# Reciprocals of an attention softmax spread over partitions by two transfers, their product moved to GpSimd, and keys spread by 8 transfers

## Chip, cores and metric

One core of one Trainium2 chip. The metric is the device time of one execution in microseconds (us), as the median of several runs.

## What is computed

Cross-attention with 16 heads of width 8 over sequences of 64 tokens (128 of them, 8192 tokens of width 128, all f32), added to its input, and then a feed-forward layer in which each token goes to the one expert of eight (each 128 to 512 to 128) that its logits choose.

```
x = x + _L0_xattn_ref(_layernorm(x), ctx, ctx, Wq, bq, Wk, bk, Wv, bv, Wo, bo)
x = x + _L0_ffn_ref(_layernorm(x), Wr, br, W1, b1, W2, b2)

q, k, v = heads(Q @ Wq.T + bq), heads(K @ Wk.T + bk), heads(V @ Wv.T + bv)
probs = softmax(einsum('bhqd,bhkd->bhqk', q, k) / sqrt(8))
out = einsum('bhqk,bhkd->bhqd', probs, v) @ Wo.T + bo

expert_idx = argmax(xf @ Wr.T + br)
h = relu(einsum('td,efd->etf', xf, W1) + b1)
y = einsum('etf,edf->etd', h, W2) + b2      # of the expert chosen
```

## The kernel before

Every engine has its own program, written out by hand; they meet at semaphores, and nothing reorders them. There are three stages.

**Stage 1** (0 to about 69 us) goes over 16 groups of 512 tokens (4 tiles of 128) and makes QT and KT (width on the partitions) and V.

**Stage 2** goes over 64 tiles in steps n, skewed by hand: in step n the scores of tile n are made, and older tiles are carried on. On TensorE a step is `scores(n)` (L877), the first four transposes of the exponentials of tile n-2 (L918) into bank 4, then small products, then the last four transposes into the same bank 4, which must wait until ScalarE has copied the first four out (L529), then the products with V (L994) and the sums of the exponentials (L1003) of tile n-3. VectorE takes the maximum (L698) and subtracts it (L706), ScalarE exponentiates (L546). GpSimd writes V out block by block (`VP`, L451) and sends routed rows to memory (L466, one indirect DMA a step).

The sums for one group of four tiles stand in one bank (tiles and heads on the partitions, the 128 queries along them), and in step 4g+7 VectorE takes their reciprocals for the whole group g (L702, `RD`). In step n, the "small products" are: `C_SEL` times RD (L948), which puts the reciprocals of tile n-8 on the 8 partitions of each head; the output projection of tile n-9 (L952); for every second tile pair the router's transposes (L977) or logits (L959). VectorE then multiplies bank 7 with the kept numerators `NUM` to `OT` (L722) and adds the projection to X (L725).

`KM` holds the keys of one group (two slots), block diagonal over the heads; 16 DMAs of 8 partitions a group put them there, from SP (L341), and for the first group from GpSimd (L410). Wait order: the KM slot of group s is free when the scores of group s-2 are made.

**Stage 3** is the feed-forward layer over 71 blocks of 128 rows, one in each step from step F0 = 67, beside the last steps (67 to 80) of stage 2. TensorE's part is L1009, L1024, L1037. SP loads each block's rows (L362). The experts' weights WE (2576 KB, L348) and W2 (2048 KB, L350) are loaded by SP late in stage 2, into places that stage 2 has given up.

Of the kernel before, what the change touches and what calls it, by code (L numbers as in the profile page):

```python
# [14 lines left out]
P = 128  # L15
# [29 lines left out]
C_ID, C_TRI, C_ONE, C_OWN, C_DEN, C_SEL, C_PREF, C_BASE, C_LIM, C_BLK, C_EPS, C_1H, C_LE, C_END = np.cumsum(  # L45
    [0, P, P, P, 2 * DK, GT * 64, GT * P, E, E, NT, NB, 1, ST, E * E]).tolist()
# [5 lines left out]
def constants():  # L52
# [12 lines left out]
    for t in range(GT):  # L65
        c[:, C_SEL + P * t:C_SEL + P * (t + 1)] = (p[:, None] // DK == p[None, :] // DK) & (p[:, None] % DK == t)
# [100 lines left out]
def build(nc, x, ctxT, wts, we, w2, con, pad, ids, out):  # L167
# [3 lines left out]
    rows = nc.dram_tensor("rows", (ROWS, RW), f32).ap()  # L171

    ctx = ExitStack()
    with ctx:
# [20 lines left out]
        BQK = W[:, W_BQ:W_BQ + 2]  # L195
        WR, BR = W[:, W_R:W_R + E], W[:, W_BR:W_BR + E]

        X1T = sb("X1T", P, 4, 2, P)
# [37 lines left out]
        RD = sb("RD", P, 2, P)  # L236
        OT = sb("OT", P, 2, P)
# [37 lines left out]
        con_in, w_in, ids_in, w2_in = sem("con_in"), sem("w_in"), sem("ids_in"), sem("w2_in")  # L275
# [15 lines left out]
        num_kept, rdx_done, wr_mm, wr_ready = (sem(n) for n in ("num_kept", "rdx_done", "wr_mm", "wr_ready"))  # L291
# [19 lines left out]
        def _(sp):  # L311

            def load_group(s):
                def go(before):
# [3 lines left out]
                    if isinstance(s.n, int) and s.n == 0:  # L318
                        sp.dma_start(C[:], con).then_inc(con_in, 16)
                        sp.dma_start(W[:], wts).then_inc(w_in, 16)  # L320
                        sp.dma_start(IDS[:], ids).then_inc(ids_in, 16)
# [10 lines left out]
            def spread(s):  # L332
                sp.wait_ge(q_kept, s.n + 1)
                sp.sem_inc(spread_go, 1)
                need(sp, s_done, GT * (s.n - 1))
                sp.sem_inc(spread_go, 1)
                at = bass.ds(s.n * GW, GW)
                for g in range(2):
                    for j in range(HP):
                        own = slice(SEQ * g + DK * j, SEQ * g + DK * (j + 1))  # L340
                        sp.dma_start(KM[own, s.r, j, :], KT[own, at]).then_inc(km_in[s.r], 16)  # L341
            steps(sp, 1, NG, 2, spread, peel=2)


            for r in range(2):
                sp.wait_ge(km_in[r], 16 * H * (NG // 2 - 1 + r))
# [22 lines left out]
            for n in range(NB1 - E):  # L369
                load_block(0)(Step(n // RR, n % RR, RR))  # L370
# [16 lines left out]
        def _(pool):  # L387
# [8 lines left out]
            def stage1(n):  # L396
# [9 lines left out]
                if 8 <= n < 12:  # L406
                    for k in range(4 * (n - 8), 4 * (n - 7)):
                        g, j = divmod(k, HP)
                        own = slice(SEQ * g + DK * j, SEQ * g + DK * (j + 1))
                        pool.dma_start(KM[own, 0, j, :], KT[own, 0:GW]).then_inc(km_first, 16)  # L410
# [24 lines left out]
            def masks(s):  # L435
                j = s.batch(M_INV[0])
# [50 lines left out]
        def _(act):  # L487
# [4 lines left out]

            def root(n, dst, src, slots, mv, sd, rstd):
                need(act, rstd, n + 1 - slots)
                act.wait_ge(mv, n + 1)
                nc.scalar.activation(dst, src, ACT.Sqrt, bias=C[:, C_EPS:C_EPS + 1]).then_inc(sd, 1)

            def keep(t):
# [11 lines left out]
                if isinstance(s.n, int) and s.n == 0:  # L510
                    act.wait_ge(w_in, 16)
# [9 lines left out]
            def softmax(s):  # L521
# [8 lines left out]
                for i in range(4):  # L530
                    j = s.batch(M_TR + 2 * i)
                    if j is not None:
                        act.wait_ge(xt2_done, 4 * j + i + 1)
                        need(act, lgp_done, 4 * j - 3 + i)
                        nc.scalar.copy(X1T[:, i].rearrange("p t d -> p (t d)"), bank(6)[:, 2 * P:4 * P]).then_inc(x1t_ready, 1)
# [45 lines left out]
        def _(dve):  # L581
# [110 lines left out]
            def stage2(s):  # L692
# [7 lines left out]
                if late == 0 and 0 <= g < NG:  # L700
                    dve.wait_ge(od_done, GT * g + GT)
                    nc.vector.reciprocal(RD[:, g % 2, :], bank(5)[:, P * (g % 2):P * (g % 2) + P]).then_inc(rd_done, 1)  # L702
# [7 lines left out]
                need(dve, rdx_done, min(n - L_MUL + 1, NT))  # L710
# [8 lines left out]
                m = n - L_MUL  # L719
                if 0 <= m < NT:  # L720
                    dve.wait_ge(num_kept, m + 1)
                    nc.vector.tensor_tensor(OT[:, m % 2, :], bank(7)[:, 0:P], NUM[:, m % 8, :], ALU.mult).then_inc(ot_ready, 1)  # L722
# [142 lines left out]
        def _(pe):  # L865
# [3 lines left out]
            nc.tensor.matmul(bank(7)[:, D:D + E], C[:, C_ONE:C_ONE + P], WR, start=True, stop=True).then_inc(wr_mm, 1)  # L869

# [12 lines left out]
            def stage1(s):  # L883
                pe.wait_ge(ct_in[s.r], 16 * (s.it + 1))
                need(pe, k_kept, s.n - 1)
                nc.tensor.matmul(bank(4 + s.r % 2), WK, CT[:, s.r, :], start=True, stop=True).then_inc(k_done, 1)
# [16 lines left out]
                if isinstance(s.n, int) and s.n == NG - 1:  # L903
                    pe.wait_ge(km_first, 16 * H)
                    scores(0)
                need(pe, q_kept, s.n - 1)
                nc.tensor.matmul(bank(2 + s.r % 2), WQ, XNT[:, s.r % 2, :], start=True, stop=True).then_inc(q_done, 1)
# [13 lines left out]
            def stage2(s):  # L921
                n = s.n
                if 1 <= n < NT:
                    grp, t = divmod(n, GT)
                    if t == 0 and grp:
                        pe.wait_ge(km_in[grp % 2], 16 * H * ((grp + 1) // 2))
# [10 lines left out]
                need(pe, ot_ready, min(n - L_MUL, NT))  # L937
# [6 lines left out]
                m = n - L_MUL  # L944
                if 0 <= m < NT:
                    g, t = divmod(m, GT)
                    pe.wait_ge(rd_done, g + 1)
# [149 lines left out]
```

## Time and profile before

| | |
|---|---|
| median of 3 runs | 499.24 us (497.53 to 502.27) |
| the profiled execution | 501.58 us, its span 499.8 us |
| busy: TensorE, VectorE | 461.1 us (92%), 408.2 us (82%) |
| busy: ScalarE, GpSimd | 313.0 us (63%), 240.6 us (48%) |
| scores of tile 0, of tile 63 | about 68 us, about 322 us |
| last matmul of the last block | about 488 us |

Half of the span is stage 2 (some 4 us a tile), a third is stage 3 (71 blocks, 1.9 us each where nothing else goes on), the rest stage 1. TensorE's busy time is modelled and is high whenever something is in its pipeline, so where it waits has to be read from the starts of its instructions.

### The profile page before, as it was taken

How to read it: one execution, taken by the hardware profiler on the slowest of the kernel's cores; microseconds unless marked ns; L12 is line 12 of the kernel's file. 1: busy time of each engine (PE TensorE's matmuls, PEld its weight loads, DVE VectorE, ACT ScalarE, POOL GpSimd, SP SyncE). 2: the span in 40 equal slices, each digit the busy share in tenths (PEclk: the TensorE clock that was granted, in tenths of full speed). 3: DMA queues.
4: the chain of work that ended last, by engine and by line, in shares of the span. 5: the costliest groups of instructions: out<-in, count | busy, mean ns of one | idle time of the engine just before them, and what ended most of it. 6: DMA issues, size and time to landing. Idle time of an engine off the chain costs nothing. (4 is left out here: it accounts for less than half of the span.)

```text
span 499.8 us, 18728 instructions
## 1 busy us (share of the span) xinstructions
PE 461.1 (92%) x6467; PEld 347.9 (70%) x6467; DVE 408.2 (82%) x1061; ACT 313.0 (63%) x589; POOL 240.6 (48%) x390
## 2 busy tenths in 40 slices
PE   3999978899999999999999999988789999999990
PEld 1666634456666666666666666668779999999990
DVE  4999864677899899998999999958878887887870
ACT  1677764666666666666666665665557777777760
POOL 1548620222232464555645645554767645455551
PEclk9999995999999999999999999999999999999996
DMA  8356300011000111111111115722223332222100
GB/s 281 108 148 177 90 11 12 14 22 20 18 17 18 33 41 30 38 38 36 35 34 33 39 41 201 264 71 76 77 66 103 101 87 66 72 61 74 39 32 0
DMA packets 32752, 33.98 MB, mean 68 GB/s; under 512 B 6675, under 2 KB 26006, under 8 KB 32416
## 3 DMA queue, kind: packets, MB, share of 16 engines
q1 hardware_dynamic: 27840, 24.10, 18.7%
q0 software_dynamic: 4832, 8.80, 5.3%
q8 instruction: 53, 0.87, 0.8%
q14 instruction: 27, 0.22, 0.2%
HBM read 19.14 MB, written 9.99 MB: 58 GB/s over the span
## 5 line engine op out<-in xcount | busy, mean ns | idle before, releaser
L451 POOL TENSOR_TENSOR VP<-BIG,C 128x128 f32<-128x128 f32 x128 | 56.1, 458 | 136.5 <-PE PS L1003 132.7
L918 PEld LDWEIGHTS PS<-C,SB 128*128 128x128 f32 x512 | 54.6, 142 | 68.2 <-ACT SB L546 32.5
L698 DVE TENSOR_REDUCE MX<-PS 128x16 f32<-128x1024 f32 x64 | 78.3, 1223 | 29.1 <-PE PS L877 27.7
L473 POOL DMA_INDIRECT out<-SB,BIG x71 | 70.1, 987 | 52.6 <-DVE SB L849 44.7
L918 PE MATMUL PS<-C,SB 128*128 128x128 f32 x512 | 85.1, 290 | 7.5 <-ACT PT L529 7.2
L546 ACT ACTIVATE SB<-SB 128x1024 f32<-128x1024 f32 x64 | 67.7, 1057 | 23.7 <-DVE SB L706 22.0
L706 DVE TENSOR_TENSOR SB<-PS,MX 128x1024 f32<-128x1024 f32 x64 | 77.4, 1210 | 1.7
L1024 PE MATMUL PS<-BIG,KM 128*128 128x128 f32 x568 | 76.8, 277 | 0.3 <-issue 0.2
L1037 PE MATMUL PS<-KM,SB 128*128 x568 | 75.8, 277 | 0.6 <-ACT SB L563 0.6
L466 POOL DMA_INDIRECT rows<-X,DESTI x64 | 64.2, 1003 | 19.6 <-issue 14.1
L877 PE MATMUL PS<-KM,BIG 64*64 64x512 f32 x512 | 71.2, 629 | 0.8 <-ACT BIG L517 0.8
L559 ACT COPY KM<-BIG 128x644 f32 x71 | 51.7, 729 | 30.2 <-PE PS L1024 24.8
L1024 PEld LDWEIGHTS PS<-BIG,KM 128*128 128x128 f32 x568 | 69.7, 192 | 1.4 <-issue 1.2
L1037 PEld LDWEIGHTS PS<-KM,SB 128*128 128x128 f32 x568 | 69.1, 192 | 1.2 <-issue 0.8
L538 ACT COPY PT<-PS 128x512 f32<-128x512 f32 x64 | 37.5, 586 | 36.7 <-PE PS L918 36.6
L529 ACT COPY PT<-PS 128x512 f32<-128x512 f32 x64 | 37.4, 585 | 36.2 <-PE PS L918 32.8
L838 DVE TENSOR_TENSOR SB<-PS,KM 128x512 f32<-128x512 f32 x71 | 49.0, 690 | 5.4 <-PE PS L1024 2.4
L563 ACT ACTIVATE SB<-SB 128x512 f32<-128x512 f32 x71 | 44.6, 628 | 10.0 <-DVE SB L838 9.7
L994 PE MATMUL PS<-PT,VP 128*32 128x64 f32 x2048 | 42.3, 223 | 0.2
L1003 PE MATMUL PS<-PT,C 128*32 128x128 f32 x1024 | 40.3, 276 | 1.1 <-DVE RD L702 0.7
L994 PEld LDWEIGHTS PS<-PT,VP 128*32 128x32 f32 x2048 | 31.9, 110 | 11.1 <-issue 11.0
L846 DVE TENSOR_TENSOR SB<-PS,KM 128x128 f32<-128x128 f32 x71 | 20.6, 291 | 18.1 <-PE PS L1037 17.2
(122 smaller groups left out, 699.0 us busy)
## 6 DMA issues: line engine op xcount, KB each, us to landing
BIG<-rows SPq DMA_DIRECT2D x71, 66.0 KB, 1.9
X<-in_x SPq DMA_DIRECT2D x16, 256.0 KB, 3.3
PT<-in_ctxT SPq DMA_DIRECT2D x16, 256.0 KB, 3.0
KM<-BIG SPq DMA_DIRECT2D x240, 16.0 KB
BIG<-in_we SPq DMA_DIRECT2D x1, 2576.0 KB, 11.5
KM<-in_w SPq DMA_DIRECT2D x1, 2048.0 KB, 15.9
out<-SB,BIG POOLq DMA_INDIRECT x71, 2.3
rows<-X,DESTI POOLq DMA_INDIRECT x64, 2.4
```

Source lines behind the costliest of these rows:

```text
L451: last = nc.gpsimd.tensor_tensor(dst, v, own, ALU.mult)
L466: nc.gpsimd.indirect_dma_start(out=rows, out_offset=bass.IndirectOffsetOnAxis(ap=DESTI[:, j % 2, t:t + 1], axis=0), in_=X[:, j * ST + t, : ...
L473: nc.gpsimd.indirect_dma_start(out=out, out_offset=bass.IndirectOffsetOnAxis(ap=RT[:, s.r, ID:ID + 1].bitcast(i32), axis=0), in_=YO[:, s.r ...
L546: nc.scalar.activation(SB[:, n % 3, :], SB[:, n % 3, :], ACT.Exp, scale=SCALE).then_inc(exp_done, 1)
L559: nc.scalar.copy(WS[:, s.r % 4, :], WE[:, bass.ds(ex, 1), :].rearrange("p e f -> p (e f)")).then_inc(ws_ready, 1)
L698: nc.vector.tensor_reduce(MX[:, n % 2, :], sc, axis=AX.X, op=ALU.max).then_inc(mx_done, 1)
L706: nc.vector.tensor_tensor(SB[:, n % 3].rearrange("p (h k) -> p h k", h=H), sc, MX[:, n % 2, :].unsqueeze(2).to_broadcast([P, H, SEQ]), ALU ...
L877: last = nc.tensor.matmul(bank(2 * (n % 2) + g)[SEQ * b:SEQ * (b + 1), :], QT[rows_g, n * P + SEQ * b:n * P + SEQ * (b + 1)], KM[rows_g, g ...
L918: last = nc.tensor.transpose(bank(4)[:, i * P:(i + 1) * P], SB[:, n % 3, hp * P:(hp + 1) * P], ident)
L994: nc.tensor.matmul(bank(6)[32 * c:32 * c + 32, at:at + SEQ], VP[:, m % 2, b, 2 * c + z, :], PT[:, m % 2, 2 * c + z, SEQ * b:SEQ * b + SEQ] ...
L1024: last = nc.tensor.matmul(bank(2 + b.r % 2)[:, c * P:(c + 1) * P], WS[:, b.r % 4, c * P:(c + 1) * P], XT[:, b.r % 2, :], start=True, stop= ...
L1037: last = nc.tensor.matmul(bank(4 + b.r % 2)[:, 0:D], HT[:, b.r % 2, c * P:(c + 1) * P], w, start=c == 0, stop=c == FC - 1)
```

## The change

- L948 and the constant `C_SEL` (256 KB of the constants) are gone. In their place SP's `ratios(g)` waits for the reciprocals of group g, writes RD (64 KB) to a scratch tensor `ratio` in memory, waits for that, and reads it back (256 KB) to `RDX` with each head's rows laid on its 8 partitions.
- The product `OT` is made by GpSimd, from RDX and NUM, at the start of its step; TensorE waits for it in the step after.
- For the read to be one run per head, the heads' layout changes: 8 DMAs of 16 partitions (every eighth) spread the keys of a group; Wq and Wk are copied with turned columns by ScalarE at the start, TensorE's first key product waits for that, and their biases come by two small DMAs.
- WE and W2 are loaded from ScalarE's queue, after the exponentials of tile 58 and tile 61; TensorE waits for W2 two steps later. `ratios(14)` stands on SP ahead of the stores of padding rows, `ratios(15)` behind the first 8 loads of blocks.

```diff
@@ SP
-            def spread(s):
-                ...
-                for g in range(2):
-                    for j in range(HP):
-                        own = slice(SEQ * g + DK * j, SEQ * g + DK * (j + 1))
-                        sp.dma_start(KM[own, s.r, j, :], KT[own, at]).then_inc(km_in[s.r], 16)
-            steps(sp, 1, NG, 2, spread, peel=2)
+            def ratios(g):
+                sp.wait_ge(rd_done, g + 1)
+                need(sp, rdx_in[g % 2], 16 * (g // 2))
+                sp.dma_start(ratio[g % 2], RD[:, g % 2, :]).then_inc(rd_out[g % 2], 16)
+                need(sp, ot_ready, GT * (g - 1))
+                sp.wait_ge(rd_out[g % 2], 16 * (g // 2 + 1))
+                of = ratio[g % 2].rearrange("(h a) q -> h a q", a=DK)[:, 0:GT, :].rearrange("h t q -> h (t q)")
+                sp.dma_start(RDX[:, g % 2].rearrange("p t q -> p (t q)"), of.unsqueeze(1).to_broadcast([H, DK, GT * P])).then_inc(rdx_in[g % 2], 16)
+
+            for s in range(1, NG):
+                ...
+                for j in range(HP):
+                    sp.dma_start(KM[j:P:HP, s % 2, j, :], KT[j:P:HP, s * GW:(s + 1) * GW]).then_inc(km_in[s % 2], 16)
+                if s >= 2:
+                    ratios(s - 2)
...
             sp.dma_start(PADR[:], pad).then_inc(padr_in, 16)
-            sp.dma_start(WE[:], we).then_inc(we_in, 16)
-            sp.wait_ge(s_done, NT - GT)
-            sp.dma_start(W2, w2).then_inc(w2_in, 16)
+            ratios(NG - 2)
             sp.wait_ge(padr_in, 16)
...
             for n in range(NB1 - E):
+                if n == 8:
+                    ratios(NG - 1)
                 load_block(0)(Step(n // RR, n % RR, RR))
@@ GpSimd
             def masks(s):
+                m = s.n - L_MUL
+                if 0 <= m < NT:
+                    g, t = divmod(m, GT)
+                    pool.wait_ge(rdx_in[g % 2], 16 * (g // 2 + 1))
+                    pool.wait_ge(num_kept, m + 1)
+                    need(pool, wo_done, m - 1)
+                    nc.gpsimd.tensor_tensor(OT[:, m % 2, :], RDX[:, g % 2, t, :], NUM[:, m % 8, :], ALU.mult).then_inc(ot_ready, 1)
@@ ScalarE
+            act.wait_ge(w_in, 16)
+            for k, w in enumerate((WQ, WK)):
+                last = nc.scalar.copy(RDX[:, 0, k, :].rearrange("p (g d j) -> p g d j", g=2, d=DK), turned(w))
+            last.then_inc(w_turned, 1)
...
                 softmax(Step(n // ST, n % ST, ST))
+                if n == NT - 6:
+                    for r in range(2):
+                        act.wait_ge(km_in[r], 16 * HP * (NG // 2 - 1 + r))
+                    act.dma_start(WE[:], we).then_inc(we_in, 16)
+                if n == NT - 3:
+                    act.wait_ge(s_done, NT - GT)
+                    act.dma_start(W2, w2).then_inc(w2_in, 16)
@@ VectorE
-                    nc.vector.tensor_tensor(OT[:, m % 2, :], bank(7)[:, 0:P], NUM[:, m % 8, :], ALU.mult).then_inc(ot_ready, 1)
@@ TensorE
+                if 0 <= n - L_X1 < NT:
+                    pe.wait_ge(ot_ready, n - L_X1 + 1)
...
-                m = n - L_MUL
-                if 0 <= m < NT:
-                    g, t = divmod(m, GT)
-                    pe.wait_ge(rd_done, g + 1)
-                    nc.tensor.matmul(bank(7)[:, 0:P], C[:, C_SEL + P * t:C_SEL + P * (t + 1)], RD[:, g % 2, :],
-                                     start=True, stop=True).then_inc(rdx_done, 1)
...
-            pe.wait_ge(w2_in, 16)
             pe.wait_ge(tab_ready, 1)
             for n in range(F0, STEPS):
                 k = n - F0
+                if k == 2:
+                    pe.wait_ge(w2_in, 16)
```

Where the instructions stand. On TensorE, one step of stage 2 in which the router's transposes are made, before:

```order
L877 MATMUL PS<-KM,BIG 64x512 x4
L918 MATMUL PS<-C,SB 128x128 x4
L948 MATMUL PS<-RD,C 128x128
L952 MATMUL PS<-W,OT 128x128
L977 MATMUL PS<-C,X 128x128 x2
L918 MATMUL PS<-C,SB 128x128 x4
L994 MATMUL PS<-PT,VP 32x64 x16
L1003 MATMUL PS<-PT,C 32x128 x8
```

The same step after (L906 is the scores, L947 the transposes, L976 the projection, L1001 the router's transposes, L1018 and L1027 the products with V and the sums):

```order
L906 MATMUL PS<-KM,BIG 64x512 x4
L947 MATMUL PS<-C,SB 128x128 x4
L976 MATMUL PS<-W,OT 128x128
L1001 MATMUL PS<-C,X 128x128 x2
L947 MATMUL PS<-C,SB 128x128 x4
L1018 MATMUL PS<-PT,VP 32x64 x16
L1027 MATMUL PS<-PT,C 32x128 x8
```

One product is gone from between the two sets of transposes; the rest stands as before. On SP, the end of stage 2 before:

```order
L347 DMA BIG<-in_pad 128x132 [waits km_in1,km_in0]
L348 DMA BIG<-in_we 128x5152
L350 DMA KM<-in_w 128x4096 [waits s_done]
L353 DMA rows<-BIG 128x132 [waits padr_in]
L353 DMA rows<-BIG 128x132 x6
```

And after, where the two weights are on ScalarE and the ratios of groups 13 and 14 stand here (those of group 15 follow behind 8 block loads):

```order
L343 DMA ratio<-RD 128x128 [waits rdx_in1,rd_done]
L347 DMA RDX<-ratio 128x1x512 [waits rd_out1,ot_ready]
L362 DMA BIG<-in_pad 128x132 [waits km_in1,km_in0]
L343 DMA ratio<-RD 128x128 [waits rdx_in0,rd_done]
L347 DMA RDX<-ratio 128x1x512 [waits rd_out0,ot_ready]
L366 DMA rows<-BIG 128x132 [waits padr_in]
L366 DMA rows<-BIG 128x132 x6
```

SP now waits in its own order for VectorE's reciprocals and for its own store, with the padding stores and the block loads queued behind.

## Rows read from the trace of the kernel before

**Rows 1.** The page: busy time by engine, share of the span, instructions.

```profile
PE 461.1 (92%) x6467; PEld 347.9 (70%) x6467; DVE 408.2 (82%) x1061; ACT 313.0 (63%) x589; POOL 240.6 (48%) x390
```

**Rows 2.** Timeline, TensorE, steps 7 to 9: start, us, line, count, [idle before].

```profile
96.45 1.09 PE L877 MATMUL PS<-KM,BIG 64*64 64x512 f32 x8
98.80 0.66 PE L918 MATMUL PS<-C,SB 128*128 128x128 f32 x4 [0.68 <-ACT PT L529]
...
100.41 1.09 PE L877 MATMUL PS<-KM,BIG 64*64 64x512 f32 x8
...
101.92 0.39 PE L948 MATMUL PS<-RD,C 128*128 128x128 f32 x2
...
104.37 1.09 PE L877 MATMUL PS<-KM,BIG 64*64 64x512 f32 x8
...
105.88 0.39 PE L948 MATMUL PS<-RD,C 128*128 128x128 f32 x2
106.10 0.39 PE L952 MATMUL PS<-W,OT 128*128 128x128 f32 x2
106.72 0.66 PE L918 MATMUL PS<-C,SB 128*128 128x128 f32 x4 [0.23 <-ACT PT L529]
```

**Rows 3.** Timeline, VectorE: maximum of tile 4 and of tile 63, 59 tiles later.

```profile
85.74 1.23 DVE L698 TENSOR_REDUCE MX<-PS 128x16 f32<-128x1024 f32 x1 [4.10 <-PE PS L877]
...
324.05 1.22 DVE L698 TENSOR_REDUCE MX<-PS 128x16 f32<-128x1024 f32 x1
```

**Rows 4.** Instructions in groups: count, then busy us, mean ns, idle before.

```profile
L451 POOL TENSOR_TENSOR VP<-BIG,C 128x128 f32<-128x128 f32 x128 | 56.1, 458 | 136.5 <-PE PS L1003 132.7 <-ACT BIG L515 3.8
L948 PE MATMUL PS<-RD,C 128*128 128x128 f32 x128 | 25.4, 280 | 3.7 <-DVE POS L681 1.5 <-DVE PREF L655 1.1 <-DVE X L725 1.0
L722 DVE TENSOR_TENSOR OT<-PS,NUM 128x128 f32<-128x128 f32 x64 | 17.9, 280 | 6.2 <-PE PS L959 3.3 <-PE PS L948 1.8 <-PE PS L968 0.7
```

**Rows 5.** DMA issues: count, KB each, median us from issue to landing.

```profile
BIG<-rows SPq DMA_DIRECT2D x71, 66.0 KB, 1.9
...
PT<-in_ctxT SPq DMA_DIRECT2D x16, 256.0 KB, 3.0
...
rows<-X,DESTI POOLq DMA_INDIRECT x64, 2.4
...
C<-in_con SPq DMA_DIRECT2D x1, 696.0 KB, 4.2
```

**Rows 6.** Timeline, VectorE: reciprocals of group 0.

```profile
98.75 0.95 DVE L702 RECIPROCAL RD<-PS 128x128 f32<-128x128 f32 x1
```

**Rows 7.** Timeline, 304 to 316 us: loads of WE and W2, ScalarE, group 13.

```profile
304.40 1.57 SPq L348 DMA_DIRECT2D BIG<-in_we  x1
...
305.28 1.06 ACT L546 ACTIVATE SB<-SB 128x1024 f32<-128x1024 f32 x1 [0.92 <-DVE SB L706]
...
306.72 4.05 SPq L353 DMA_DIRECT2D rows<-BIG  x7
...
307.71 0.95 DVE L702 RECIPROCAL RD<-PS 128x128 f32<-128x128 f32 x1
...
315.31 0.30 PEld L952 LDWEIGHTS PS<-W,OT 128*128 128x128 f32 x2
```

**Rows 8.** Line 466 (GpSimd's row store), the one issued at 305.9 us.

```profile
DMA to landing us min/median/max: 7.5/7.5/7.5
```

**Rows 9.** Timeline, 325 to 343 us: reciprocals of groups 14 and 15, projections in steps 65 and 69, block loads.

```profile
325.18 0.95 DVE L702 RECIPROCAL RD<-PS 128x128 f32<-128x128 f32 x1
...
326.80 17.47 SPq L362 DMA_DIRECT2D BIG<-rows  x16
...
331.21 0.30 PEld L952 LDWEIGHTS PS<-W,OT 128*128 128x128 f32 x2
...
337.00 0.95 DVE L702 RECIPROCAL RD<-PS 128x128 f32<-128x128 f32 x1
...
342.21 0.30 PEld L952 LDWEIGHTS PS<-W,OT 128*128 128x128 f32 x2
```

More of the change, by code:

```diff
@@ L194, in build, with turned @@
         BO = W[:, W_BO:W_BO + D]
-        BQK = W[:, W_BQ:W_BQ + 2]
+        BQK = sb("BQK", P, 2)
+        def turned(w):
+            return w.rearrange("p (g j d) -> p g d j", g=2, j=HP)
         WR, BR = W[:, W_R:W_R + E], W[:, W_BR:W_BR + E]
-        X1T = sb("X1T", P, 4, 2, P)
+        X1T = sb("X1T", P, 2, 2, P)
         STAT2, MS2 = sb("STAT2", P, ST, 6), sb("MS2", P, 4, ST)
@@ L236, in build @@
         RD = sb("RD", P, 2, P)
+        RDX = sb("RDX", P, 2, GT, P)
         OT = sb("OT", P, 2, P)
@@ L290, in build @@
         stat2, mv2, inv_step, scaled = (sem(n) for n in ("stat2", "mv2", "inv_step", "scaled"))
-        num_kept, rdx_done, wr_mm, wr_ready = (sem(n) for n in ("num_kept", "rdx_done", "wr_mm", "wr_ready"))
+        num_kept, wr_mm, wr_ready = (sem(n) for n in ("num_kept", "wr_mm", "wr_ready"))
+        rd_out, rdx_in = sems("rd_out", 2), sems("rdx_in", 2)
         seed_step, sd2_done, inv2_done = sem("seed_step"), sem("sd2_done"), sem("inv2_done")
@@ L320, in go @@
                         sp.dma_start(W[:], wts).then_inc(w_in, 16)
+                        for g in range(2):
+                            own = slice(SEQ * g, SEQ * (g + 1))
+                            sp.dma_start(BQK[own, :], wts[own, W_BQ:W_BQ + 2].rearrange("(j d) b -> d j b", j=HP)).then_inc(b_in, 16)
                         sp.dma_start(IDS[:], ids).then_inc(ids_in, 16)
@@ L406, in stage1 @@
                 if 8 <= n < 12:
[L407 to L410, printed above, removed]
+                    for j in range(2 * (n - 8), 2 * (n - 7)):
+                        pool.dma_start(KM[j:P:HP, 0, j, :], KT[j:P:HP, 0:GW]).then_inc(km_first, 16)
             for n in range(NG):
@@ L533, in softmax @@
                         act.wait_ge(xt2_done, 4 * j + i + 1)
-                        need(act, lgp_done, 4 * j - 3 + i)
-                        nc.scalar.copy(X1T[:, i].rearrange("p t d -> p (t d)"), bank(6)[:, 2 * P:4 * P]).then_inc(x1t_ready, 1)
+                        need(act, lgp_done, 4 * j - 1 + i)
+                        nc.scalar.copy(X1T[:, i % 2].rearrange("p t d -> p (t d)"), bank(6)[:, 2 * P:4 * P]).then_inc(x1t_ready, 1)
                 if 2 <= n < NT + 2:
@@ L885, in stage1 @@
                 need(pe, k_kept, s.n - 1)
-                nc.tensor.matmul(bank(4 + s.r % 2), WK, CT[:, s.r, :], start=True, stop=True).then_inc(k_done, 1)
+                nc.tensor.matmul(bank(4 + s.r % 2), RDX[:, 0, 1, :], CT[:, s.r, :], start=True, stop=True).then_inc(k_done, 1)
                 pe.wait_ge(xn_done, s.n + 1)
@@ L903, in stage1 @@
                 if isinstance(s.n, int) and s.n == NG - 1:
-                    pe.wait_ge(km_first, 16 * H)
+                    pe.wait_ge(km_first, 16 * HP)
                     scores(0)
                 need(pe, q_kept, s.n - 1)
-                nc.tensor.matmul(bank(2 + s.r % 2), WQ, XNT[:, s.r % 2, :], start=True, stop=True).then_inc(q_done, 1)
+                nc.tensor.matmul(bank(2 + s.r % 2), RDX[:, 0, 0, :], XNT[:, s.r % 2, :], start=True, stop=True).then_inc(q_done, 1)
             steps(pe, 0, NG, 4, stage1, peel=4, tail=4)
@@ L958, in stage2 @@
                             at = 2 * P + (ST * (j % 2) + 2 * i + t) * E
-                            last = nc.tensor.matmul(bank(7)[:, at:at + E], X1T[:, i, t, :], WR, start=True, stop=True)
+                            last = nc.tensor.matmul(bank(7)[:, at:at + E], X1T[:, i % 2, t, :], WR, start=True, stop=True)
                         last.then_inc(lgp_done, 1)
```

27 lines of the change are left out of this document (11 added, 16 removed).

## Prediction

> **What bounds the kernel now.** Start with the page's busy times: TensorE and VectorE lead [rows 1], and half of the span is the 64 attention tiles. TensorE's busy share says little here, so I read the starts of its instructions. Step 7 has neither L948 nor L952 and lasts 100.41 - 96.45 = 3.96 us; step 8 has L948 and lasts 104.37 - 100.41 = 3.96 us [rows 2]. The reader is to see why: between the two sets of transposes stands the copy out of bank 4. TensorE waits 0.68 us for it in step 7 with nothing in the gap, and still 0.23 us in step 9 with both L948 and L952 in it. What fills the gap is free. So 3.96 us is a floor made of TensorE's long products and one round trip to ScalarE, and neither VectorE nor L948 is in it.
>
> How much lies above the floor? From the maximum of tile 4 to that of tile 63 are 324.05 - 85.74 = 238.3 us [rows 3]; 59 steps at 3.96 are 233.6. **4.7 us** is all that relief of VectorE or of the gap can give in stage 2.
>
> **The change part by part.**
>
> *L948 and L722 go.* By their durations that is 25.4 us of TensorE and 64 x 0.28 = 17.9 us of VectorE [rows 4]. By the argument above most of it is slack. VectorE loses 0.28 us a step, more than it lags, and the full steps of the router lose L948 from a gap that was over-full there. I take 4.0 of the 4.7 us, bounds 2 and 4.7. In steps 64 to 71 TensorE has no scores, and in the steps with blocks it goes from one product to the next, so L948 counts there: the next product starts 106.10 - 105.88 = 0.22 us after it [rows 2]; 8 x 0.22 = 1.8 us, bounds 1 and 3. What is late next once L722 is gone is OT itself, from GpSimd.
>
> *Start.* 256 of the 696 KB of constants go, which landed after 4.2 us [rows 5]; taking 1.9 us of it as fixed, as a 66 KB load takes in all, 256/696 x 2.3 = 0.85 us. The loads behind on SP, which the first statistics and so TensorE's first transposes wait for, land that much sooner. Against it stand two small bias DMAs on SP ahead of these loads and two ScalarE copies before the first key product, both shorter than the wait for data. I take 0.8, bounds 0 and 1.
>
> *The chain of a group in the steady state.* Reciprocals of group 0 end at 98.75 + 0.95 = 99.70 [rows 6]. The first projection that needs them is L952 of step 9; with L948 gone it could start 0.22 us sooner than at 106.10, at 105.88 [rows 2]. That leaves 6.2 us, plus about 0.4 us for which it can be late unseen, because the gap is not full. In it must go: the store of 64 KB, the load of 256 KB, and GpSimd's product. The nearest rows are the 66 KB block load, 1.9 us, and the context load of 256 KB to 128 partitions, 3.0 us [rows 5]; the product lies between 0.28 us (VectorE's) and 0.46 us (GpSimd's L451 on as many elements) [rows 4]; I take 0.46. With 0.3 us for three wake-ups the sum is 1.9 + 3.0 + 0.46 + 0.3 = 5.7 us against 6.6. **Hidden, with 0.9 us to spare.** Were the store as slow as GpSimd's row store, 2.4 us, it would be 6.2, still hidden. This is the closest call of the whole forecast, since 13 groups would pay any excess.
>
> The row for a store is 2.4 us and for loads 1.9 and 3.0. The Trainium skill (DMA: Bandwidth & Descriptors, "Anatomy of one DMA") has about 2.0 us fixed, most of it the receipt of the write and worst into HBM, plus bytes over 436 GB/s: an estimate from it is 2.15 + 2.6 = 4.75 us for the two transfers, where the rows give 4.9. By either the chain is hidden.
>
> *GpSimd.* It is busy 48% [rows 1]; 64 x 0.46 = 29 us more fit. Its product stands ahead of VP in the step, and VP is needed two steps later; while it waits for RDX, VP, the reciprocal square root of the router and the row stores are queued behind it, all with more than a step of slack. Cost 0, bounds 0 and 1.
>
> *Keys by 8 transfers.* SP has fewer to issue, and the keys of a group are issued before its ratios come due, with four steps of lead. Cost and gain 0.
>
> *WE from ScalarE.* Before, its issue took 1.57 us on SP, where nobody cared [rows 7]. Now it stands behind the exponentials of tile 58 (305.28 + 1.06 = 306.34) and ahead of the next step's copy L529, which is the round trip of the floor and followed at once. If the issue starts when the exponential ends, TensorE loses 1.5 us; if it is issued under the exponential, 0.5. I take 1.2. W2's issue comes once more in that place: 0.2.
>
> *Group 13 crosses the load of WE.* A row store of GpSimd issued as WE's load began took 7.5 us to land, not 2.4 [rows 5, 8]: 5.1 us more. The reciprocals of group 13 end at 308.66 and L952 is at 315.31 [rows 7]; 6.65 us, plus 1.2 for ScalarE's issue, minus 0.22, plus 0.2 of slack are 7.8. The chain is 5.7 us plus what the store is held back: 4.5 to 5.1. The load back is then past WE. 5.7 + 4.6 - 7.8 = 2.5 us of stall, bounds 0 and 5. The row store is a small transfer on a queue of its own, and yet it was held back by 5.1 us [rows 5, 8]. The Trainium skill (DMA: Bandwidth & Descriptors, "Queues, rings and completion order") has each DMA engine take turns between queues packet by packet, by which a small transfer would lose little and the stall would be near 0; the 7.5 us speak against it here, and it is the mechanism of the rival below that ends faster.
>
> *Group 14.* Reciprocals end at 326.13, L952 of step 65 is at 331.21 [rows 9]: 5.1 us, minus 0.2 and plus 0.3 against a chain of 5.7, and W2, issued some 3 us before, still lands: stall 1.0, bounds 0 and 4.
>
> *Group 15.* On SP stand ahead of it the 7 padding stores (4.05 us [rows 7], so some 3 us in quiet) behind the ratios of group 14, and then 8 block loads at 17.47 / 16 = 1.09 us [rows 9]. The store of group 14 is out about 3 us after its reciprocals: 329.4; plus 3 plus 8.7 = 341. The reciprocals end at 337.95 [rows 9], so SP is 3 us late. Chain: 341 + 5.7 = 346.8 against L952 at 342.21 (and the tail ahead of it is about 1 us shorter, while the stalls shift both sides alike). Some of SP's lateness shrinks as the stalls push the reciprocals back. Taken 3.5, bounds 1.5 and 5.5. Nobody hides it: TensorE has all later blocks behind that product.
>
> **Sum.** Gains 4.0 + 1.8 + 0.8 = 6.6; losses 1.2 + 0.2 + 2.5 + 1.0 + 3.5 = 8.4; net **+1.8 us**. Against the profiled execution, 501.58 us, that is 503.4; that execution was 2.3 us above the median of the three runs, 499.24, so the forecast of the median is **501.0**, its own range 496 to 505. 1% is 5 us; that is about what a measurement of this kernel can tell from no change.
>
> **Rivals.**
>
> *Faster: the crossings are cheap.* If transfers take turns and ScalarE issues under its exponential, groups 13 and 14 cost nothing and WE 0.3; group 15 costs 1.5 to 2. Sum -6.6 + 2 = -4.6, about 494.5; half of this case is beyond 1%. For it: the stretch is short. Against: the 7.5 us row.
>
> *Slower: the chain is longer than the slack in every group.* Its place is the wait for OT in steps 4g+9. It decides at 6.6 us. If store and load back (eight readers of the same row, never seen in the trace) take 6.7 us instead of 4.9, the stall is 0.9 us in each of 13 groups: +12 us, about 513; at 0.4 us excess 506.
>
> *Slower: the end costs double.* The upper bounds of groups 13 to 15 together with ScalarE's issue: 1.6 + 5 + 4 + 5.5 = 16, less 6.6: +9.5 us, about 508.
>
> *The change gives VectorE's and TensorE's durations in full.* If the floor were VectorE's, 17.9 us would go from stage 2: about 485. The two equal steps speak against it plainly.
>
> **Chances.** Forecast 0.48, crossings cheap 0.18, chain too long 0.13, end double 0.18, in full 0.03. Faster by over 1%: half of the second, the last, and a little of the first: 0.18. Slower by over 1%: 0.29 of the two slow cases and a little of the first: 0.32. Within: 0.50. The range takes in both slow cases but for their ends and the cheap case: 493 to 511.
>
> **What would show it.** Stage 2's steady step still 3.96 us (right) or shorter (wrong floor). In steps 4g+9 no idle time of the projection on GpSimd (right), or some 1 us in each (chain too long). A wait of TensorE on OT in step 61, and the longest in step 69; a gap on ScalarE at tile 58. If stage 2 from tile 4 to tile 57 is not shorter by 2 to 3 us, the first term is wrong.

## The result and the profile after

The changed kernel takes **525.46 us** in the median of 6 runs (524.81 to 533.62); the kernel before, in the same sessions, 499.21 us (497.53 to 502.52). The ratio is 1.053, 95% interval 1.049 to 1.056: 26 us slower, where 501.0 was predicted and the range ended at 511. The profiled execution took 525.42 us, its span is 523.6 us, and its mean granted clock is 0.966. Medians and ranges, here and below, are over all runs, while the ratios leave out runs in a slower state (one of the 6 here, one of 4 in number 3, two of 6 in number 6, one of 12 in number 12).

One remark on the text ahead of the prediction: it says that the layout of the heads is changed so that the read back is one run per head. That is wrong. The read of a head's ratios was one run already; the turned columns of Wq and Wk serve the keys, so that 8 transfers with every eighth partition can spread them. It also leaves out that X1T, the buffer of the router's transposed input, goes from four slots to two; number 2 below has that too and shows no cost.

The page's busy times, to be held against [rows 1]:

```profile
PE 455.9 (87%) x6339; PEld 340.1 (65%) x6339; DVE 397.8 (76%) x997; ACT 312.4 (60%) x591; POOL 264.0 (50%) x446
```

TensorE and VectorE have 5 and 10 us less to do, GpSimd 23 us more, and the kernel is 26 us longer: nothing in busy time says why. So the same first step as before: maxima of tiles on VectorE (timeline; start, us, line), for [rows 3], here of tiles 4 and 63.

```profile
82.30 1.22 DVE L730 TENSOR_REDUCE MX<-PS 128x16 f32<-128x1024 f32 x1 [1.48 <-PE PS L906]
...
339.59 1.22 DVE L730 TENSOR_REDUCE MX<-PS 128x16 f32<-128x1024 f32 x1
```

257.3 us for the 59 steps, against 238.3. By the same maxima (of tiles 0, 4, 16, 56 and 63), in us:

| | tile 0 | tile 4 | 4 to 16 | 16 to 56 | 56 to 63 | 63 to end of span |
|---|---|---|---|---|---|---|
| before | 69.1 | 85.7 | 47.5 | 160.7 | 30.1 | 175.8 |
| after | 69.6 | 82.3 | 48.6 | 170.5 | 38.2 | 184.0 |

Three places lose: 10 us over tiles 16 to 56, 8 us in the last seven steps, 8 us in the tail. (Tile 4 is earlier because TensorE ran at 1.2 GHz from 75.3 to 85.5 us in that execution of the kernel before, and not in this one; number 5 below has such a stretch again.) Steps of 3.96 us are still the rule; but between tiles 16 and 56 one in eight lasts 6.1 to 7.8 us, and one of the last seven 10.7. The view of waits (engine, what, released by; total us, times, longest) names them:

```profile
POOL OT L455 <- DMA RDX<-ratio: 45.6, 15, 9.0
...
DVE PREF L687 <- POOL X L444: 20.2, 6, 6.6
...
PE PS L976 <- DVE PREF L687: 15.8, 7, 6.4
...
DVE X L753 <- PE PS L976: 7.6, 2, 4.1
...
PE PS L976 <- POOL OT L455: 7.1, 5, 4.7
```

L976 is the projection, L455 GpSimd's product, L444 the last operation of a Newton step on GpSimd (the router needs a reciprocal square root, which GpSimd finds by Newton's method, in twelve small operations for 8 tiles, six in each of two steps), L687 the first operation of the router's ranking on VectorE. The direct wait of the projection for the product, on which the forecast watched, is 7.1 us. More than twice that comes round by VectorE: the projection stands behind the ranking in TensorE's order, the ranking waits for the Newton steps, and these stand on GpSimd behind the product that waits for its transfer. One such place in the timeline, 249 to 257 us:

```profile
249.37 0.55 SPq L347 DMA_DIRECT2D RDX<-ratio  x1
...
252.61 0.44 POOL L455 TENSOR_TENSOR OT<-RDX,NUM 128x128 f32<-128x128 f32 x1 [3.56 <-DMA RDX<-ratio]
253.02 0.19 POOL L441 TENSOR_TENSOR YY<-C,YY 128x8 f32<-128x8 f32 x1
...
254.41 0.21 POOL L444 TENSOR_TENSOR X<-YY,Y 128x8 f32<-128x8 f32 x1
...
254.75 0.23 DVE L687 TENSOR_TENSOR PREF<-PS,X 128x64 f32<-128x64 f32 x1 [3.95 <-POOL X L444]
...
255.12 0.46 PE L976 MATMUL PS<-W,OT 128*128 128x128 f32 x2 [2.73 <-DVE PREF L687]
...
256.36 1.08 PE L1018 MATMUL PS<-PT,VP 128*32 128x64 f32 x32
```

The product waits 3.56 us for the load; six small Newton operations follow in 1.6 us; then VectorE and TensorE go on at once. The product itself was not late for TensorE: OT was there at 253.05, two microseconds before the projection began. And the last row shows a second price: L1018 takes 1.08 us instead of 0.65, because TensorE ran at 1.2 GHz from 256.3 to 259.8 us, just after the gap. The router's batches come every 8 tiles and meet the first product of every second group, so this happens at 152, 186, 220, 255, 289 and 329 us. The place shown is the longest of the first five, since the store of this group took 3.1 us and not 1.6 (see the last section); at the others TensorE waits 0.98 to 1.49 us.

Group 13 and the load of WE (timeline, 312 to 329 us), for [rows 7]:

```profile
312.53 1.06 ACT L571 ACTIVATE SB<-SB 128x1024 f32<-128x1024 f32 x1 [0.76 <-DVE SB L739]
312.59 0.40 ACTq L596 DMA_DIRECT2D BIG<-in_we  x1
...
315.48 0.95 DVE L735 RECIPROCAL RD<-PS 128x128 f32<-128x128 f32 x1
...
316.45 0.33 SPq L343 DMA_DIRECT2D ratio<-RD  x1
...
323.26 0.55 SPq L347 DMA_DIRECT2D RDX<-ratio  x1
...
326.55 0.44 POOL L455 TENSOR_TENSOR OT<-RDX,NUM 128x128 f32<-128x128 f32 x1 [7.21 <-DMA RDX<-ratio]
...
328.36 0.21 POOL L444 TENSOR_TENSOR X<-YY,Y 128x8 f32<-128x8 f32 x1
...
329.07 0.77 PE L976 MATMUL PS<-W,OT 128*128 128x128 f32 x2 [6.38 <-DVE PREF L687]
```

Two things to see. WE's issue takes 0.40 us and lies under the exponential, so ScalarE lost nothing by it. And the store took 6.7 us, as foreseen; but TensorE is freed by the same detour, 2.5 us after the product began, and its wait is 6.38 us. The tail, group 15 (timeline, 353 to 364 us), for [rows 9]:

```profile
354.30 0.95 DVE L735 RECIPROCAL RD<-PS 128x128 f32<-128x128 f32 x1
...
358.32 0.37 SPq L343 DMA_DIRECT2D ratio<-RD  x1
360.02 0.56 SPq L347 DMA_DIRECT2D RDX<-ratio  x1
...
363.29 0.44 POOL L455 TENSOR_TENSOR OT<-RDX,NUM 128x128 f32<-128x128 f32 x1 [8.98 <-DMA RDX<-ratio]
...
363.99 0.77 PE L976 MATMUL PS<-W,OT 128*128 128x128 f32 x2 [4.75 <-POOL OT L455]
```

SP is 3.07 us late, as the prediction had it. Around these gaps the granted clock is down (stretches; busy by engine, then PEclk, DMA share, GB/s); before, all stretches from 320 to 400 us have 1.00:

```profile
320.00:330.00 10.00, 3.62 (x65) 2.40 (x65) 3.20 (x11) 2.38 (x4) 2.82 (x10) 0.73 0.23 78
330.00:340.00 10.00, 9.91 (x149) 6.14 (x147) 7.88 (x19) 5.07 (x10) 5.36 (x9) 0.76 0.62 226
340.00:350.00 10.00, 7.84 (x175) 5.96 (x175) 5.43 (x15) 5.22 (x12) 5.34 (x12) 1.00 0.34 102
350.00:360.00 10.00, 6.35 (x83) 5.56 (x83) 5.62 (x20) 4.70 (x10) 3.93 (x5) 0.77 0.35 83
360.00:380.00 20.00, 16.01 (x120) 15.81 (x121) 12.18 (x45) 9.62 (x22) 12.85 (x16) 0.78 0.31 82
```

### The profile page after: what moved, and what is told of

Same layout as the page of the kernel before. It is cut to its first block and busy times, and to the rows that moved or that the text cites. A ratio compares the mean times of both kernels' runs of the same rounds, so it can differ in the third digit from the quotient of the medians.

```text
span 523.6 us, 18138 instructions
## 1 busy us (share of the span) xinstructions
PE 455.9 (87%) x6339; PEld 340.1 (65%) x6339; DVE 397.8 (76%) x997; ACT 312.4 (60%) x591; POOL 264.0 (50%) x446
## 5 line engine op out<-in xcount | busy, mean ns | idle before, releaser
L947 PEld LDWEIGHTS PS<-C,SB 128*128 128x128 f32 x512 | 54.5, 141 | 75.7 <-ACT SB L571 29.1
L947 PE MATMUL PS<-C,SB 128*128 128x128 f32 x512 | 83.9, 287 | 14.9 <-ACT PT L554 12.6
L1048 PE MATMUL PS<-BIG,KM 128*128 128x128 f32 x568 | 78.7, 281 | 0.1
L1048 PEld LDWEIGHTS PS<-BIG,KM 128*128 128x128 f32 x568 | 71.5, 196 | 1.2 <-issue 0.9
L906 PE MATMUL PS<-KM,BIG 64*64 64x512 f32 x512 | 71.1, 628 | 0.8 <-ACT BIG L542 0.8
L455 POOL TENSOR_TENSOR OT<-RDX,NUM 128x128 f32<-128x128 f32 x64 | 29.5, 461 | 50.5 <-DMA RDX<-ratio 45.6
L976 PE MATMUL PS<-W,OT 128*128 128x128 f32 x128 | 27.2, 295 | 23.9 <-DVE PREF L687 15.8
L1018 PE MATMUL PS<-PT,VP 128*32 128x64 f32 x2048 | 42.7, 225 | 0.9
L1027 PE MATMUL PS<-PT,C 128*32 128x128 f32 x1024 | 41.1, 278 | 1.5 <-DVE RD L735 1.4
```

The costliest lines, as they stand in the source:

```text
L906: last = nc.tensor.matmul(bank(2 * (n % 2) + g)[SEQ * b:SEQ * (b + 1), :], QT[rows_g, n * P + SEQ * b:n * P + SEQ * (b + 1)], KM[rows_g, g ...
L947: last = nc.tensor.transpose(bank(4)[:, i * P:(i + 1) * P], SB[:, n % 3, hp * P:(hp + 1) * P], ident)
L1048: last = nc.tensor.matmul(bank(2 + b.r % 2)[:, c * P:(c + 1) * P], WS[:, b.r % 4, c * P:(c + 1) * P], XT[:, b.r % 2, :], start=True, stop= ...
```

## The experiments

Each kernel was timed beside the kernel before; the ratio is to that. Edits are to the changed kernel where nothing else is said, and shortened, with the cuts marked `...`. "Rest" is the last column of the table above.

**1. The product behind Newton's steps.** In GpSimd's step:

```diff
-                m = s.n - L_MUL
-                if 0 <= m < NT:
...
                 j = s.batch(M_INV[1])
                 if j is not None and j < JS:
                     pool.wait_ge(seed_step, 4 * j + 4)
                     newton(j, 6, INV_STEPS)
+                m = s.n - L_MUL
+                if 0 <= m < NT:
+                    ...
```

> One edit to the changed kernel: in GpSimd's step the product OT stands behind the Newton iterations of the router's reciprocal root, no longer ahead of them. Theory A (GpSimd's order): the second half of Newton stands behind a product that waits for RDX, and VectorE (PREF) and through it TensorE wait for Newton; then stage 2 loses about 1.5 us in each of 6 batches of 8 steps less, and the clock falls less often: 511 to 517 us against 525.5. Theory B (the transfers are simply too long): the wait for RDX stays where it is, TensorE waits for OT instead: 523 to 526.

Measured 515.50 us (514.09 to 516.81), ratio 1.033 (1.030 to 1.036): 10 us less by one block of lines moved. In the profiled execution tiles 16 to 56 went from 170.5 to 162.3 us and the last seven steps from 38.2 to 36.1. In its view of waits:

```profile
POOL OT L462 <- DMA RDX<-ratio: 43.4, 16, 8.0
...
PE PS L976 <- DVE PREF L687: 2.0, 1, 2.0
```

GpSimd waits for the transfers as long as ever; what has gone is who waited behind it. This shows the detour, and leaves 16 us.

**2. No transfers.** The product waits for VectorE's reciprocals and multiplies by them as they stand; both transfers are gone, and the spread with them.

```diff
-ratios(...)
...
-pool.wait_ge(rdx_in[g % 2], 16 * (g // 2 + 1))
+pool.wait_ge(rd_done, g + 1)
-nc.gpsimd.tensor_tensor(OT[..], RDX[:, g % 2, t, :], NUM[..], ALU.mult)
+nc.gpsimd.tensor_tensor(OT[..], RD[:, g % 2, :], NUM[..], ALU.mult)
```

> The changed kernel without the two transfers of a group: GpSimd multiplies straight from RD, so the reciprocals are not spread over the partitions (this part of the computation is left out). The product stays on GpSimd, the weights stay on ScalarE's queue. Theories A and B both have every loss behind the wait for RDX: 491 to 497 us, with 3.96 us a step, faster than the kernel before by its 6 us of lag and tail. Theory C (GpSimd's 29 us of products, or the loads of weights from ScalarE, cost by themselves): 505 or more.

Measured 499.88 us (497.74 to 504.27), ratio 1.002 (0.999 to 1.005). All the loss hangs on the transfers and what waits for them; GpSimd's product alone costs nothing that can be seen. But no theory had it right: by both the relief of TensorE and VectorE should have brought 491 to 497, and it did not.

**3. The product back on VectorE**, from RDX, at its old place; the transfers stay, and GpSimd's product goes.

```diff
+                    dve.wait_ge(rdx_in[g % 2], 16 * (g // 2 + 1))
+                    ...
+                    nc.vector.tensor_tensor(OT[:, m % 2, :], RDX[:, g % 2, t, :], NUM[:, m % 8, :], ALU.mult)
```

> The changed kernel with the product back on VectorE, read from RDX and standing where it stood before the change; the transfers stay. Theory A: Newton is free on GpSimd, PREF does not wait, but VectorE now waits for RDX itself in step 4g+8, behind its subtraction and with a step to go: 508 to 516 us. Theory B: 522 or more. A third, that the move to GpSimd is what costs: near 500.

Measured 525.97 us (521.11 to 530.04), ratio 1.052 (1.046 to 1.057). Theory A missed here by 10 us; the time lies in the range of theory B, which number 1 had already ruled out as the whole cause. An engine that waits for a transfer in the middle of its order costs as much on VectorE as on GpSimd; in its view of waits VectorE's product has 28.1 us, where after had 20.2 us of VectorE's waiting for Newton. So, with number 1, it is the place of the wait in an order, not the engine.

```profile
DVE OT L750 <- DMA RDX<-ratio: 28.1, 13, 6.3
```

**4. The keys alone.** The kernel before with the 8 key transfers, the turned weights and the bias loads.

```diff
-for g in range(2):
-    for j in range(HP):
-        ...
-        sp.dma_start(KM[own, s.r, j, :], KT[own, at])...
...
+for j in range(HP):
+    sp.dma_start(KM[j:P:HP, s % 2, j, :], KT[j:P:HP, s * GW:(s + 1) * GW])...
...
```

> The kernel before with one part of the change: keys spread by 8 transfers of 16 partitions, with the turned weights, the ScalarE copies and the two bias loads (the turned weights stand in NUM, free in stage 1). All theories: 497.5 to 501, no change beyond 1 us at the start. If the turned weights or the DMAs with every eighth partition cost something of their own, 502 or more.

Measured 497.95 us (497.11 to 501.73), ratio 0.998 (0.996 to 1.001): no difference that can be told.

**5. The last ratios earlier on SP**, ahead of the third block load.

```diff
-                if n == 8:
+                if n == 2:
                     ratios(NG - 1)
```

> The changed kernel with the store and load of the last group's reciprocals ahead of the third block load on SP instead of the ninth. In the changed kernel that store went out 3.07 us after its reciprocals and TensorE then waited 4.75 us at L976, after which 13.7 us ran at half clock. Theory S (SP's order is the price of the tail): the store goes out at once, the wait falls to about 2 us and the half-clock stretch may go: 3 to 7 us less, 518 to 522. Theory X (the group is late by its chain and its wait on GpSimd anyway, the order on SP is a detail): 524 to 526.

Measured 524.46 us (522.43 to 525.74), ratio 1.050 (1.046 to 1.053): 1 us, theory X by the median. The store now goes out at once, and yet L976 waits 3.66 us, for VectorE now, which waited 2.79 us for the rows of a block; on SP the block loads stand behind the store's receipt instead:

```profile
357.19 0.33 SPq L343 DMA_DIRECT2D ratio<-RD  x1
...
362.26 0.42 DVE L860 TENSOR_SCALAR BIG<-BIG 128x128 f32<-128x128 f32 x1 [2.79 <-DMA BIG<-rows]
...
363.57 0.76 PE L976 MATMUL PS<-W,OT 128*128 128x128 f32 x2 [3.66 <-DVE POS L713]
```

The profiled executions show more than the median: the rest is 181.0 us against 184.0, so the edit is worth 3.0 us where it acts, with 3.4 us at 1.2 GHz there and not 13.7. This execution gave the gain back ahead of tile 4, which it reached 4.6 us later, behind 10.2 us at 1.2 GHz.

**6. The weights from SP**, as before, instead of from ScalarE.

```diff
             sp.dma_start(PADR[:], pad).then_inc(padr_in, 16)
+            sp.dma_start(WE[:], we).then_inc(we_in, 16)
+            sp.wait_ge(s_done, NT - GT)
+            sp.dma_start(W2, w2).then_inc(w2_in, 16)
             ratios(NG - 2)
...
-                if n == NT - 6:
-                    ...
-                    act.dma_start(WE[:], we).then_inc(we_in, 16)
-                if n == NT - 3:
-                    ...
-                    act.dma_start(W2, w2).then_inc(w2_in, 16)
```

> The changed kernel with the loads of WE and W2 issued by SP where the kernel before has them (behind the padding's load, ahead of the ratios of group 14) instead of by ScalarE. Theory E (ScalarE's issue costs a microsecond, and the crossing stays since WE's load still begins within some us of the reciprocals of group 13): 523 to 525. Theory W (by SP the load of WE goes out before the store of group 13 by more than now, so that the store does not wait 6.7 us, and 11.9 us of step and 10 us at half clock go with it): 514 to 520. SP now waits for the scores of tile 60 ahead of the ratios of group 14, at no cost by either.

Measured 522.28 us (516.50 to 527.47), ratio 1.041 (1.035 to 1.046). Against the changed kernel that is 3.2 us less by the medians and 6.0 by the ratios (1.041 against 1.053). The median lies between the two theories; the ratios and the trace speak for W: the store of group 13 took 3.1 us, the seven last steps 33.7 us instead of 38.2.

**7. All three edits**, by the diffs of numbers 1, 5 and 6.

> The changed kernel with all three edits: GpSimd's product behind Newton's steps, the last ratios ahead of the third block load, WE and W2 from SP. If the three costs (Newton behind the product, 10 us as measured; the end of SP's queue, 3 to 7; the crossing, 0 to 8) are all there is and they add, 500 to 508; with the crossing unmoved 508 to 513. A rival, that one cost hides the others and the tail's remainder is that GpSimd is in TensorE's way at all, has it above 511.

Measured 505.08 us (504.67 to 507.17), ratio 1.012 (1.009 to 1.015). One by one they gave 10.0, 1.0 and 3.2 us by the medians, 14.2 in all, and together 20.4. By the ratios it is 10.0, 1.5 and 6.0, 17.5 in all, against 20.5, and 3 us are within what the intervals of these ratios allow. So it isn't shown that each edit hides behind another.

**8. Only L948 left out.** The kernel before without the spread; VectorE multiplies by RD as it stands.

```diff
-need(dve, rdx_done, ...)
...
-nc.tensor.matmul(bank(7)[:, 0:P], C[:, C_SEL + P * t:C_SEL + P * (t + 1)], RD[:, g % 2, :], ...)
...
-nc.vector.tensor_tensor(OT[..], bank(7)[:, 0:P], NUM[..], ALU.mult)
+nc.vector.tensor_tensor(OT[..], RD[:, (m // GT) % 2, :], NUM[..], ALU.mult)
```

> The kernel before, which leaves the spread of the reciprocals over the rows out: no L948, and VectorE multiplies the numerators by the reciprocals as they stand (that part of the result is left out). It is the price of L948 alone. The prediction's working (what lies above the floor goes, 2 to 4.7 us, and 8 x 0.22 in the tail) gives 493 to 496. The rival from the run without transfers, which had 499.88: there is nothing to gain from the gap, 497 to 500; then GpSimd's product costs nothing either, while 493 to 496 would say that GpSimd's product gave the gain back.

Measured 500.56 us (497.95 to 503.35), ratio 1.002 (1.000 to 1.005): 128 products of TensorE taken away, and nothing gained. Tiles 16 to 56 take 159.8 us, 0.9 less than before; tiles 56 to 63 take 30.6, 0.5 more; the rest is 178.8, 3.0 more, with the clock down in that execution in a tail where the kernel before has 1.00:

```profile
330.00:340.00 10.00, 7.20 (x128) 6.20 (x117) 6.14 (x26) 5.33 (x11) 4.00 (x5) 0.78 0.39 98
340.00:350.00 10.00, 9.65 (x63) 9.68 (x64) 6.88 (x29) 5.20 (x11) 6.27 (x8) 0.71 0.16 50
```

**9. Number 8 with idle products** in the last eight steps, in L948's place, read by nobody.

```diff
+if NT - 2 * GT <= n - L_MUL < NT:
+    nc.tensor.matmul(bank(7)[:, 0:P], C[:, C_ONE:C_ONE + P], C[:, C_ID:C_ID + P], start=True, stop=True)
```

> The kernel before without the spread (as the run with only L948 left out), and in its last eight steps a product of the same size, ones by identity, in the place where L948 stood; nothing reads it. With only L948 left out, stage 2 was 3 us shorter up to tile 56 but the rest after tile 63 was 178.8 us against 175.8, and TensorE ran at 1.2 GHz from 335.6 to 345.8 us, where the kernel before has 2.4 GHz. Theory C (the products in the gaps of the tail keep the clock, and their removal costs it): the rest falls back to about 176, 2.4 GHz throughout the tail, 496 to 498. Theory N (the clock there falls in some executions whatever stands in the gap): no steady difference, 499 to 501.

Measured 499.99 us (496.53 to 501.26), ratio 1.001 (0.998 to 1.003). The profiled execution is the one that theory C describes, 175.4 us of rest and the clock at 1.00:

```profile
330.00:340.00 10.00, 7.39 (x107) 6.64 (x107) 8.29 (x33) 6.17 (x13) 3.96 (x5) 1.00 0.36 90
340.00:350.00 10.00, 10.00 (x93) 10.00 (x92) 8.44 (x35) 6.82 (x14) 7.56 (x9) 1.00 0.24 69
```

But it is one of twelve, and the median does not follow. The listed clocks of all executions tell more. The 59 of the kernel before lie on a line: 5 at a mean clock of 0.981 to 0.982 took 502.2 us on average, 17 at 0.991 to 0.992 took 498.1. Against a line through those 59, number 8 (mean clock 0.981) is 0.9 us faster at equal clock, number 9 (0.985) 0.8 and number 2 (0.983) 0.7, each with a standard error of 0.1 to 0.3. The kernel before has 0.987. So L948's relief is worth 0.9 us, which is what tiles 16 to 56 show, and a lower clock takes it back. That the idle products raised it from 0.981 to 0.985 speaks for theory C; it is not settled.

**10. Number 7 with the idle products**, by the diff of number 9.

> The changed kernel with the three edits together (product behind Newton's steps, last ratios ahead of the third block load, weights from SP), which took 505.08 us, and the same idle product in the last eight steps. Theory C: some of the 10 us at 1.2 GHz between 332 and 349 us goes, 501 to 504. Theory N, or waits of 2 and 3.6 us before the falls that a product of 0.3 us does not bridge: 504 to 507.

Measured 508.60 us (507.04 to 510.16), ratio 1.017 (1.014 to 1.020): 3.5 us slower than number 7, outside both theories, at the same mean clock (0.981). That the idle products cost this isn't shown: of the 4.0 us between the two profiled executions 2.9 lie ahead of tile 63, where no idle product stands yet, and 1.1 in the rest. They were no remedy, and could hardly be one. They stand behind TensorE's wait for OT and not in it, so the wait stays (the idle product waits 1.91 and 3.62 us for groups 14 and 15, where number 7's projection waits 1.96 and 3.56), and the projection starts 0.3 to 0.6 us after them.

**11. Numbers 1 and 6 together**, by their two diffs.

> Two of the three edits: GpSimd's product behind Newton's steps and the weights from SP, the last ratios behind eight block loads as in the changed kernel. One by one the edits gave 10.0, 1.0 (order of the last ratios) and 3.2 us (weights), together 20.4. If the weights' load crossing group 13 is what remained beside Newton: 505 to 509, and the order of the last ratios is worth 0 to 3. If the last ratios' order needs the other two to show: 510 to 513.

Measured 509.55 us (507.05 to 511.39), ratio 1.018 (1.015 to 1.022). Beside number 1 the weights' queue is worth 6.0 us by the medians (7.2 by the ratios). Beside these two the order of the last ratios is worth 4.5 (3.2 by the ratios), where number 5's median had 1.0. In the profiled executions the rest is 184.9 us here and 181.7 in number 7: 3.2 us, about the 3.0 of number 5. So this edit gives some 3 us both alone and beside the others.

**12. Number 7 without transfers for the last two groups** (the spread of tiles 56 to 63 is left out).

```diff
-                    pool.wait_ge(rdx_in[g % 2], 16 * (g // 2 + 1))
+                    if g < NG - 2:
+                        pool.wait_ge(rdx_in[g % 2], 16 * (g // 2 + 1))
+                    else:
+                        pool.wait_ge(rd_done, g + 1)
...
+                    nc.gpsimd.tensor_tensor(OT[..], RDX[:, g % 2, t, :] if g < NG - 2 else RD[:, g % 2, :], NUM[..], ALU.mult)
```

> The three edits together, and the last two groups without transfers: GpSimd multiplies the numerators of tiles 56 to 63 by the reciprocals as they stand, so the spread of those eight tiles is left out. The three edits alone took 505.08 us, with waits of 1.96 us (group 14) and 3.56 us (group 15) at L972 and 181.7 us behind tile 63, against 175.8 before. If all that remains of the loss is these two groups' transfers: 498.5 to 501. If GpSimd's product itself holds up the tail: 502 to 505.

Measured 501.76 us (498.85 to 507.01), ratio 1.003 (1.000 to 1.005): 3.3 us less than number 7 (4.5 by the ratios), just above its theory's 498.5 to 501 and below the rival's 502 to 505.

**Together**, as a ladder from the changed kernel down, by the medians and in brackets by the ratios: GpSimd's order 10.0 us (10.0); WE's load against group 13's store 6.0 (7.2); SP's order for group 15 4.5 (3.2); what is left of groups 14 and 15 3.3 (4.5); what is left of the other transfers 1.9 (0.3). The last is number 2, which has GpSimd's order and the weights' queue of the changed kernel, so that neither costs anything where nothing waits for a transfer. That is 25.6 (25.3) of the 26 us. Each step is known to some 2 to 2.5 us only, by the intervals of the two ratios, and the last can't be told from nothing. No version was measurably faster than the kernel before.

## Why the prediction was wrong

**The step that failed** is *GpSimd*: "VP, the reciprocal square root of the router and the row stores are queued behind it, all with more than a step of slack. Cost 0, bounds 0 and 1." The reciprocal square root has no such slack: VectorE's ranking waits for it, and TensorE's projection stands behind that. The prediction named what was queued behind the wait, but did not follow the second name to its own readers; number 1 puts 10 us on it. None of the rivals was this one: "the chain is longer than the slack in every group" has the price (513, at 12 us) but puts the wait at the product, where tiles 16 to 56 have 0.42 us in all.

**The chain in the steady state** was right. In group 0 the reciprocals end at 96.27 and the product starts at 101.16 us: 4.9 us, against 1.9 + 3.0 + 0.3 = 5.2 predicted up to there; store 1.6, load 3.2, product 0.46 us. The prediction's second estimate, 2.15 + 2.6 us, had the sum right and not the split. As groups (issues: count, KB, median us to landing), beside [rows 5]:

```profile
RDX<-ratio SPq DMA_DIRECT2D x16, 256.0 KB, 3.2
...
ratio<-RD SPq DMA_DIRECT2D x16, 64.0 KB, 1.6
```

"Hidden" held for TensorE, and not for GpSimd, whose wait in each group is just this chain minus its own slack.

**Relief of L948 and L722**, 4.0 + 1.8 us, measured 0.9 for L948 (number 8 at equal clock). The floor of 3.96 us was right. The 4.7 us above it were not TensorE's gap: in number 8 the last seven steps still take 30.6 us, 2.9 above seven times the floor, and steps of 4.3 us stay. The 8 x 0.22 of the tail are not seen in any run: TensorE waits there for the router anyway ([rows 4] has L948 idle behind VectorE's L681, L655 and L725, which said so).

**Start**, 0.8 us gained: not seen. The maximum of tile 0 is at 69.64 instead of 69.11 us, and in the nine other kernels made from the changed one at 68.5 to 70.6.

**WE from ScalarE**, 1.2 + 0.2 us, measured 0 as an issue: 0.40 us under the exponential. Nor is the 1.57 us of [rows 7] what this load costs on SP: in numbers 6 to 12 SP issued it in 0.42 to 0.43 us.

**Group 13**: the crossing was right in mechanism and size (store held back by 5.1 us, 6.7 against 1.6), the wait was not: 6.38 us against 2.5, as Newton's steps stand between, and the 10.2 us at 1.2 GHz begin within it. The rival "crossings are cheap" falls with the row of 6.7 us. In the first 3.45 us after the store's issue (316.45 to 319.9 us; queue: packets, MB, share of 16 engines) its queue q1 has no row at all:

```profile
q10 hardware_dynamic: 63, 1.30, 89.7%
q0 software_dynamic: 25, 0.07, 4.9%
```

WE's load on ScalarE's queue q10 is 128 packets of 20.6 KB, 8 on average for each of the 16 DMA engines, and 108 of them have started when the first of the store's 128 small packets does, at 319.9 us. (The packets on q0 are of GpSimd's row store, issued at 313.31 us; the first of them starts at 317.7.) The Trainium skill (DMA: Bandwidth & Descriptors, "Queues, rings and completion order") has a DMA engine take turns between queues, but drain a whole packet of some 9 to 17 descriptors (the single pieces of a transfer) before it turns. The prediction took from this that a small transfer loses little, which doesn't follow: if each of the trace's packets is one descriptor, WE's 8 on an engine fit into one such packet, and the trace would agree. Whether that is the cause was not tried.

**Group 14** 0.63 us against 1.0; **group 15** 4.75 against 3.5, SP late by 3.07 against 3, both inside the bounds.

**The clock** had no term at all. In the profiled execution after, 27.3 us of the span ahead of the last matmul are at 1.2 GHz, before 10.2. The mean clock of the 6 runs is 0.964, against 0.987. Carried on along the line of the 59 executions (3.6 us for each 0.01), 0.023 is some 8 us of the 26; an estimate, since no execution of the kernel before reached so low (0.981), and it is not beside the terms above but within them, since the clock fell around those gaps. The first of the three stretches begins 1.2 us after the gap of 2.73 us, the second within that of 6.38 us, the third at 355.3 us between waits of L976 of 1.99 and 0.90 us, and it holds the 4.75 us of group 15.

**Two sums** of the prediction's rivals don't come out as written: "the end costs double", 9.5 us above 499.24, is 508.7 and not 508, and 485 for "in full" has no working; 17.9 + 1.8 + 0.8 us of gains against 8.4 of losses give 487. Neither moves the forecast.

## What to carry to other kernels

When an instruction with a long wait is put into an engine's order, follow every instruction behind it to its readers and on to the bounding engine, not only the new result to its own reader; here the new result came in time, and six unrelated 8-column operations behind it cost 10 us. Move such a product behind all work that others wait for before judging the transfer's length. And price a stall twice: the wait itself, and the clock that the rows show after it; relief that only makes gaps longer may give nothing.

## What the runs showed of the hardware

The same 64 KB store took 1.6 us in the median and up to 6.7. The line of the store (all 16), and the issues and queues around the store of group 9, which took 3.1 us:

```profile
DMA to landing us min/median/max: 1.5/1.6/6.7
```

```profile
q8 instruction: 1, 0.02, 1.7%
...
ratio<-RD SPq DMA_DIRECT2D x1, 64.0 KB, 3.1
```

In five groups (1, 2, 6, 9 and 10) the load back was issued 2.4 to 3.5 us after the store, not 1.6, and in each an instruction packet of queue q8 lies in that time, 0.9 to 1.4 us long on one of the 16 DMA engines. The other traces bear this out. Nine kernels have these transfers, with 138 stores beside the four that cross WE's load from ScalarE's queue. In 64 of them the load back came 1.9 to 3.7 us after the store, and every one of these has an instruction packet in its time; in the other 74 it came after 1.5 to 1.7 us, and none of these has one in its first 1.3 us. That the one causes the other was not tried. In group 1 it was enough for a direct wait of 1.08 us and a step of 5.00 us, the only one of its kind outside the router's steps: the 0.9 us to spare of the prediction are less than this scatter.
